# Node attention: remainders on GpSimd, fold and sines in a head's first step, one share product on ScalarE, masks on two groups of rows

## The reference, cut to what matters

```python
logits = (x @ wr).reshape(B, N, H, K_NODES).transpose(0, 2, 1, 3)
tk_vals, tk_idx = jax.lax.top_k(logits, TOP_K)
tk_w = jax.nn.softmax(tk_vals, axis=-1)
member = jax.nn.one_hot(tk_idx, K_NODES).sum(axis=-2) > 0
pos = jnp.cumsum(m_i, axis=2) - m_i                 # m_i: member as int
for n in range(K_NODES):
    c, s = cos_c[pos[..., n]], sin_c[pos[..., n]]
    qr = q * c + _rotate_half(q) * s
    kr = k * c + _rotate_half(k) * s
    scores = jnp.einsum('bhid,bhjd->bhij', qr, kr) * SCALE
    scores = jnp.where(causal & member[..., n][:, :, None, :], scores, NEG)
    outs.append(jnp.einsum('bhij,bhjd->bhid', jax.nn.softmax(scores, axis=-1), v))
gathered = jnp.take_along_axis(jnp.stack(outs, axis=3), tk_idx[..., None], axis=3)
y = (tk_w[..., None] * gathered).sum(axis=3)
```

## Time and profile before

| What | Before |
|---|---|
| median of 3 runs | 1853.75 us |
| runs | 1850.45 to 1855.61 us |
| the profiled execution's own time | 1856.05 us |
| its span | 1854.3 us |
| mean granted TensorE clock | 0.855 |
| busy: PE / DVE / ACT / POOL | 1372.8 / 1114.4 / 714.3 / 384.8 us |
| steps of the node attention | from 54 to 492 us |
| DVE busy from 102 to 158 us | 52.09 of 56 us |
| PE, ACT, POOL busy there | 48.56, 35.23, 34.30 us |

### The profile page before, as it was taken

One profiled execution on the slowest core, in us unless ns is written; L12 is line 12 of the kernel. 1 busy time (PEld: TensorE's weight loads), 2 busy tenths in 40 slices (PEclk: granted clock), 3 DMA queues, 4 the chain that ended last, 5 costly groups with the idle time before them and its releaser, 6 DMA issues. The chain is left out here.

```text
span 1854.3 us, 24940 instructions
## 1 busy us (share of the span) xinstructions
PE 1372.8 (74%) x8853; PEld 1037.9 (56%) x8853; DVE 1114.4 (60%) x2412; ACT 714.3 (39%) x1537; POOL 384.8 (21%) x400
## 2 busy tenths in 40 slices
PE   4898898888866897674674975758735977868785
PEld 3676666666745565561453964545623764744662
DVE  5899998999545576324556536443436648435634
ACT  4456666656313464232231221004102425645451
POOL 2565566665210100110101310000001000000000
PEclk8899899998878799796786986759967997989897
DMA  6011011010010100340002510000020002000100
GB/s 219 22 42 38 25 42 36 27 42 15 1 59 1 35 1 1 122 137 0 1 13 76 173 52 1 1 1 1 1 91 0 1 1 44 2 1 5 40 2 12
DMA packets 31611, 63.97 MB, mean 35 GB/s; under 512 B 6785, under 2 KB 18177, under 8 KB 30977
## 3 DMA queue, kind: packets, MB, share of 16 engines
q1 hardware_dynamic: 30464, 60.15, 10.5%
q0 software_dynamic: 1024, 2.23, 0.5%
HBM read 54.13 MB, written 4.18 MB: 31 GB/s over the span
## 5 line engine op out<-in xcount | busy, mean ns | idle before, releaser
L188 POOL TENSOR_TENSOR rstd<-spread,minus_half 128x4 f32<-128x4 f32 x36 | 36.8, 1023 | 1001.9 <-DVE spread L170 1001.9
L918 PE MATMUL l0h_scores<-l0h_k_rot,l0h_q_slots 128*128 128x128 f32 (+1 forms) x1024 | 206.6, 349 | 0.0
L918 PEld LDWEIGHTS l0h_scores<-l0h_k_rot,l0h_q_slots 128*128 128x128 f32 x1024 | 169.9, 208 | 13.1
L1135 POOL TENSOR_TENSOR l0h_k_part<-large_weights,l0h_sines 128x512 f32<-128x512 f32 x64 | 83.9, 1311 | 177.2 <-PE l0h_scores L918 129.1
L1009 ACT ACTIVATE l0h_scores<-l0h_scores,l0h_top 128x128 f32<-128x128 f32 (+1 forms) x256 | 100.4, 392 | 27.9 <-DVE l0h_top L1088 27.7
L1082 DVE TENSOR_TENSOR l0h_q_slots<-l0h_q_rot,l0h_chosen 128x1024 f32<-128x1024 f32 x64 | 78.4, 1225 | 6.7
L894 PE MATMUL l0h_projected<-XT,l0h_wq 128*128 128x256 f32 x256 | 70.2, 398 | 15.3 <-ACT large_weights L980 12.0
L908 PE MATMUL l0h_scores<-l0h_key_masks,l0h_query_picks 4*128 4x128 bf16 (+1 forms) x256 | 45.0, 257 | 49.2 <-DVE l0h_probs L1105 49.1
L1136 POOL TENSOR_TENSOR l0h_k_rot<-large_weights,l0h_cosines 128x512 f32<-128x512 f32 x64 | 80.9, 1264 | 0.0
L1088 DVE TENSOR_REDUCE l0h_top<-l0h_scores 128x2 f32<-128x256 f32 (+1 forms) x128 | 65.1, 548 | 6.4 <-PE l0h_scores L918 6.4
L1447 ACT ACTIVATE l0n_probs<-l0n_scores,l0n_top 128x256 f32<-128x256 f32 x128 | 53.8, 483 | 39.0 <-DVE l0n_top L1478 38.9
(11 more groups left out here) (762 smaller groups left out, 3585.8 us busy)
## 6 DMA issues: line engine op xcount, KB each, us to landing
l1e_experts<-in_l_experts SPq DMA_DIRECT2D x16, 768.0 KB, 4.3
l0e_experts<-in_l_experts SPq DMA_DIRECT2D x15, 578.0 KB, 4.0
l0h_chosen<-l0h_chosen_dram SPq DMA_DIRECT2D x64, 128.0 KB, 2.9
small_weights<-in_w_l_ffn SPq DMA_DIRECT2D x1, 4016.0 KB, 12.1
l0h_pos<-l0h_pos_dram SPq DMA_DIRECT2D x56, 64.0 KB, 2.0
large_weights<-in_w_l_xattn SPq DMA_DIRECT2D x1, 2632.0 KB, 9.0
l3f_late<-l3f_values SPq DMA_DIRECT2D x2, 1040.0 KB, 7.0
l0h_wq<-in_l_wq SPq DMA_DIRECT2D x16, 128.0 KB, 2.9
```

Source lines behind the costliest of these rows:

```text
L918: mm = nc.tensor.matmul(at[:, slot], q_slots[:, s % 2, slot, part, i * P:(i + 1) * P], k_rot[:, s % 2, part, 0:KEYS[i][1]], start=False, s ...
L1135: nc.gpsimd.tensor_tensor(k_part[:], source, at_batch(sines, s), ALU.mult)
```

## The change

Four edits, all in `l0_attn_heads`.

1. `reduce_turns` moves from VectorE to GpSimd for heads 2 to 15. Its place is behind `rotate_k(s)` in the first step of a head (b = 0), for head h+1; before, VectorE did it after step b = 3 for head h+2. Heads 0 and 1 stay on VectorE, ahead of the loop.
2. ScalarE does `fold(h+1)` right ahead of `sines_of(h+1)` at b = 0 and no longer at b = 3.
3. `combine` is split. `find_share(s)` (reciprocal and share) stands ahead of the slot product, which becomes `pick_slots(s+2)`. The first slot's product becomes two ScalarE copies with the share as scale, `scale_first(s)`, behind `exponents(s)` and ahead of `copy_out` and `copy_turned`. VectorE's second product waits for each of them. The two semaphores for this are ones that later attention stages use too, so their bases are raised.
4. `key_masks` and `query_picks` exist twice, at partitions 0 to 3 and 64 to 67, with a DMA each. The four mask products of a step are all issued ahead of the causal masks, with the two tiles, on different rows, taking turns.

```diff
-                    sp.dma_start(key_masks[:, h % 2], absent_dram[h * NODES:(h + 1) * NODES])\
...
+                    for i in range(TB):
+                        sp.dma_start(key_masks[rows_of_tile(i), h % 2], absent_dram[h * NODES:(h + 1) * NODES])\
+                            .then_inc(masks_loaded[h % 2], 16)
...
-                    pe.wait_ge(masks_loaded[h % 2], 32 * (h // 2 + 1))
+                    pe.wait_ge(masks_loaded[h % 2], 64 * (h // 2 + 1))
+                    for slot in range(CHOICES):
+                        for i in range(TB):
+                            query = slice((TB * b + i) * P, (TB * b + i + 1) * P)
+                            rows = rows_of_tile(i)
+                            nc.tensor.matmul(unit(scores, s, i)[:, slot], query_picks[rows, h % 2, slot, query],
+                                             key_masks[rows, h % 2, b * S:b * S + KEYS[i][1]], start=(slot == 0),
+                                             stop=False, skip_group_check=True)
...
+                def scale_first(s):
+                    act.wait_ge(shared, s + 1)
+                    if s >= 2:
+                        act.wait_ge(turned_ready, s - 1)
+                    for i in range(TB):
+                        nc.scalar.activation(prob(s, i), unit(scores, s, i)[:, 0], ACT.Copy,
+                                             scale=share[:, s % 2, i, 0:1]).then_inc(scaled, 1)
...
                     exponents(s)
+                    scale_first(s)
...
                     if b == 0 and 1 <= h < H0 - 1:
+                        fold(h + 1)
                         sines_of(h + 1)
                     if b == 2 and h + 2 < H0:
                         turns(h + 2)
-                    if b == 3 and h + 2 < H0:
-                        fold(h + 2)
...
+                def find_share(s):
                     h, b = step(s)
                     v.wait_ge(exp_ready, 2 * (s + 1))
                     link(v, nc.vector.reciprocal(inverse(s), total[:, s % 2]))
...
+                def combine(s):
                     for i in range(TB):
+                        v.wait_ge(scaled, 2 * s + i + 1)
+                        last = nc.vector.scalar_tensor_tensor(prob(s, i), unit(scores, s, i)[:, 1],
+                                                              share[:, s % 2, i, 1:2], prob(s, i), ALU.mult, ALU.add)
...
                     find_top(s)
                     if s + 2 < STEPS:
                         rotate_q(s + 2)
+                    find_share(s)
+                    if s + 2 < STEPS:
+                        pick_slots(s + 2)
                     combine(s)
-                    if b == 3 and h + 2 < H0:
-                        reduce_turns(h + 2)
...
+                def reduce_turns(h):
+                    g.wait_ge(turns_ready, h + 1)
+                    link(g, nc.gpsimd.tensor_scalar(sines[:, h % 2], cosines[:, h % 2], ROUND, ROUND, ALU.add, ALU.subtract))
+                    nc.gpsimd.tensor_tensor(sines[:, h % 2], sines[:, h % 2], cosines[:, h % 2], ALU.subtract)\
+                        .then_inc(turns_reduced, 1)
...
                 for s in range(STEPS):
+                    h, b = step(s)
                     rotate_k(s)
+                    if b == 0 and 1 <= h < H0 - 1:
+                        reduce_turns(h + 1)
```

More of the change, by code:

```diff
@@ L789, in l0_attn_heads @@
         chosen = sb("chosen", [P, 2, CHOICES, N], BF16)
-        key_masks = sb("key_masks", [NODES, 2, N], BF16)
-        query_picks = sb("query_picks", [NODES, 2, CHOICES, N], BF16)
+        key_masks = sb("key_masks", [P // 2 + NODES, 2, N], BF16)
+        query_picks = sb("query_picks", [P // 2 + NODES, 2, CHOICES, N], BF16)
+        rows_of_tile = lambda i: slice(i * P // 2, i * P // 2 + NODES)
         cosines, sines = sb("cosines", [P, 2, N]), sb("sines", [P, 2, N])
@@ L817, in l0_attn_heads @@
         inverse = lambda s: scores[:, s % 2, CHOICES * P:CHOICES * P + TB * CHOICES].rearrange("p (i o) -> p i o", i=TB)
+        share_ready, first_scaled = k.counted("attention", "shifted out_used")
+        shared, scaled = share_ready.sem, first_scaled.sem
+        prob = lambda s, i: probs[:, s % 2, i * P:i * P + KEYS[i][1]]
         with nc.Block() as block:
@@ L902, in score @@
                         pe.wait_ge(combined, s - 1)
-                    pe.wait_ge(masks_loaded[h % 2], 32 * (h // 2 + 1))
+                    pe.wait_ge(masks_loaded[h % 2], 64 * (h // 2 + 1))
[6 more added lines that the diff above has]
+                                             stop=False, skip_group_check=True)
                     for i in range(TB):
                         at = unit(scores, s, i)
-                        query = slice((TB * b + i) * P, (TB * b + i + 1) * P)
-                        for slot in range(CHOICES):
-                            nc.tensor.matmul(at[:, slot], query_picks[:, h % 2, slot, query],
-                                             key_masks[:, h % 2, b * S:b * S + KEYS[i][1]], start=(slot == 0), stop=False,
-                                             skip_group_check=True)
                         nc.tensor.matmul(at[:, :, i * P:(i + 1) * P], k.above[:], bc(k.masker[:].unsqueeze(1), [P, 2, P]),
@@ L1079, in rotate_q, with pick_slots @@
                     nc.vector.tensor_tensor(q_rot[:, 1], q_rot[:, 1], q_part[:, 0], ALU.add).then_inc(q_rotated, 1)
+                def pick_slots(s):
                     v.wait_ge(chosen_loaded[step(s)[0] % 2], 64 * (step(s)[0] // 2 + 1))
@@ L1089, in find_top @@
                             .then_inc(topped, 1)
-                def combine(s):
+                def find_share(s):
                     h, b = step(s)
@@ L1094, in combine @@
                     link(v, nc.vector.reciprocal(inverse(s), total[:, s % 2]))
-                    link(v, nc.vector.tensor_tensor(share[:, s % 2], inverse(s), mix[:, TB * b:TB * b + TB, h, :],
-                                                    ALU.mult))
-                    if s >= 2:
-                        v.wait_ge(turned_ready, s - 1)
-                    prob = lambda i: probs[:, s % 2, i * P:i * P + KEYS[i][1]]
-                    for i in range(TB):
-                        last = nc.vector.tensor_scalar(prob(i), unit(scores, s, i)[:, 0], share[:, s % 2, i, 0:1], None,
-                                                       ALU.mult)
-                    link(v, last)
-                    for i in range(TB):
-                        last = nc.vector.scalar_tensor_tensor(prob(i), unit(scores, s, i)[:, 1], share[:, s % 2, i, 1:2],
-                                                              prob(i), ALU.mult, ALU.add)
+                    nc.vector.tensor_tensor(share[:, s % 2], inverse(s), mix[:, TB * b:TB * b + TB, h, :], ALU.mult)\
+                        .then_inc(shared, 1)
+                def combine(s):
+                    for i in range(TB):
+                        v.wait_ge(scaled, 2 * s + i + 1)
+                        last = nc.vector.scalar_tensor_tensor(prob(s, i), unit(scores, s, i)[:, 1],
+                                                              share[:, s % 2, i, 1:2], prob(s, i), ALU.mult, ALU.add)
                     last.then_inc(combined, 1)
@@ L1110, in _ @@
                 reduce_turns(1)
-                rotate_q(0)
-                rotate_q(1)
+                for s in range(2):
+                    rotate_q(s)
+                    pick_slots(s)
                 for s in range(STEPS):
@@ L1145, in _ @@
                 for s in range(STEPS):
+                    h, b = step(s)
                     rotate_k(s)
+                    if b == 0 and 1 <= h < H0 - 1:
+                        reduce_turns(h + 1)
+        share_ready.base += STEPS
+        first_scaled.base += TB * STEPS
 HX, DX = 16, P // 16
```

7 lines of the change are left out of this document (3 added, 4 removed).

## The result

The changed kernel takes 1944.35 us (median of 6 runs, 1938.92 to 1947.96) against 1851.62 of six runs of the kernel before on the same chip: a ratio of 1.0485, 95% interval 1.0467 to 1.0503. It is slower, as forecast, but by 93 us and not by 31, and outside the range. Its profiled execution took 1945.9 us with a span of 1943.9, 89.6 more than before, at a mean granted clock of 0.828 against 0.855.

The account below looks back on a forecast made before the run. VectorE's 6.17 us step was taken to bound the kernel. After the change, 14 heads of 27.9 us through four queues plus 2.2 for the clock, 6.6 for heads 3, 7, 11, less 5.5 elsewhere: +30.7, about 1884 us, range 1846 to 1910.

Parts of the forecast that it names:

- VectorE's step: VectorE's own work per node attention step: from 6.17 us to 5.2, with ScalarE's two copies costed at nothing.
- The masks: TensorE's four mask products, on different rows by pairs, overlap partly: 0.15 us off an iteration.
- TensorE's turn: TensorE's score, weigh and turn at b = 2 end at T + 4.5 us; T is the end of combine(4h-3).
- The remainders: GpSimd's reduce_turns, held until turns is made: tensor_tensor 2.35 us plus tensor_scalar 1.0, together 3.4 us.
- Score, weigh, turn: TensorE's rest of score(4h+1), weigh and turn, after its stall for the rotated k: about 4.05 us with hand-over.
- The clock: Falls to 1.2 GHz behind TensorE's idle stretch cost 2.2 us a head; bounds 0, and 4 with a second fall.
- ScalarE's block: ScalarE's copy 0.5 us, fold 1.0, then first table load through sines to the reciprocal awaiting exponents, 6.45.
- TensorE's wait for combine: TensorE, done with its next iteration at T + 23.85 us, idles until T + 27.9: 4.0 us in every head.
- Outside the 14 heads: The six other full steps (0, 1, 58 to 61) gain 0.9 us each: -5.5 us.
- Rival 1: The turn through the queues holds but the clock's falls cost nothing: +0.2 us, 1854; chance 0.08.
- Rival 2: GpSimd's remainders don't hold up rotate_k: 25.45 us a head, 1850 us with the clock's 2.2, 1819 without; chance 0.16.
- Rival 3: Slower still: tensor_scalar at 2.35 us adds 19 us, a second clock fall up to 25: 1903 to 1928; chance 0.14.

Follow-up runs that it names:

- e12: The changed kernel with the split of combine undone, the first share product on VectorE again behind the slot product: 1947.86 us.
- e11: The changed kernel with only turns(h + 2) on ScalarE moved from b = 2 to b = 1: 1848.92 us.
- e2: The changed kernel with the remainders (reduce_turns) still on GpSimd but one step later, at b = 1 instead of b = 0: 1838.11 us.
- e7: The kernel before with only the doubled masks and their new order added: 1845.71 us against 1856.19.
- e4: The changed kernel with GpSimd's tensor_scalar cut from add and subtract to one multiplication, leaving out the rounding: 1939.88 us.
- e13: The changed kernel with unused TensorE products in both waits, 16 ahead of the masks of b = 1's score, 14 ahead of a head's first projection: 1908.15 us.
- e3: The changed kernel with unused TensorE products in both waits, 16 behind the masks of b = 1's score, 14 ahead of a head's first projection: 1900.38 us.
- e1: The changed kernel with the remainders (reduce_turns) back on VectorE behind step b = 3: 1868.5 us.
- e5: The changed kernel with only the 16 unused TensorE products ahead of the masks of b = 1's score, in the wait for k_rot: 1934.56 us.
- e6: The changed kernel with only the 14 unused TensorE products ahead of the projection of a head's first step: 1926.08 us.
- e8: The kernel before with the split of combine and the doubled masks, remainders and fold left at b = 3: 1842.35 us against 1856.19.

## Why the prediction was right in its sign and wrong in its size

The mechanism of the forecast holds: a loop through four queues, which VectorE enters only with the 2.2 us from reciprocal to combine's end (e12), which the changed kernel's timelines show link by link, and which e11 and e2 open by moving a single step. Point by point:

- **VectorE's step**: forecast 5.2 us, measured 5.07. ScalarE's two copies were costed at nothing: VectorE waited 0.9 us for them in all. Right.
- **The masks**: forecast 0.15 us off an iteration, measured 0.3 (e7).
- **TensorE's turn** at T + 4.5 was T + 6.7: 2.2 us, which is the clock's fall at half speed and belongs to its term.
- **The remainders**, forecast 3.4 us: 6.0. This is the first failed step, "It reads one input, not two, so I take 1.0". The tensor_tensor was right to 5 ns (2350 and 2345), the tensor_scalar 3.63. Not only the value chosen was off: the upper bound, a tensor_tensor at 2.35, was none. A two-input operation bounds a one-input one only if the inputs set the price. e4 shows that the operations do too, and that one operation alone is above the bound. 2.63 us x 14 = 37 us.
- **rotate_k** 4.0 us: 249.35 to 253.31. Right. The idle stretch of TensorE in front of it was 5.23 us in place of 2.65, and 2.65 + 2.63 = 5.28: by the dearer remainders. This is the path that the prediction had, with one link longer.
- **Score, weigh, turn** in 4.05: 5.7, the second fall.
- **The clock**, forecast +2.2 us a head with 4 kept as the bound "if the 2.65 us stall draws a second fall": the stall did, at 5.23 us. e13 against the change gives 4.0 us in each ordinary head. This is the second failed step: a term of 2.2 that should have been 4.0, 1.8 x 14 = 25 us. In heads 3, 7 and 11 no run measured it by itself, since there the added products cost time of their own. They take 35.6, 38.8 and 35.6 us; the forecast 27.9 + 2.2 + 2.2 = 32.3 and the 2.63 leave 0.6, 3.8 and 0.6, in the mean 1.7. In head 7 the clock is at 1.2 GHz for some 7 us behind each of its waits, in the other two for some 3.
- **ScalarE's block** from table load to reciprocal, 6.45 us: 260.63 to 267.08, 6.45. The copy and the fold before it, 1.5: 259.07 to 260.63. Reciprocal to T + one turn, 2.3: 2.2. Right.
- **TensorE's wait for combine**, 4.0 us: 4.26. Right.
- **Outside the 14 heads**: forecast -5.5, measured -8.0.

The two failed steps add up on the links. Forecast +30.7; the tensor_scalar adds 37 and the clock 25, outside gains 2.5 more, and 30.7 + 37 + 25 - 2.5 = 90, against 89.6 on the spans. As prices of their own they don't come apart: e4 took 0.86 us off the tensor_scalar and got 0.25 a head back in ordinary heads, since more of the clock's fall then lay on work. So the 37 us say where the time stands in the changed kernel, not what a cheaper tensor_scalar would give back.

The rivals. Rival 1, the falls cost nothing, is out by e3 and e13. Rival 2, GpSimd's remainders don't hold up rotate_k, is out by e2: 106 us go when they stand a step later. Its price was nearly right as a price of something else: it put 25.45 us on a head without that link and without the clock, and in e2 and e11 ordinary heads run at 25 to 28, with falls of the clock among them. Rival 3 had the mechanism, both of its parts came, and it still ended at 1928, because its first part was capped at the bound that failed. What I gave 0.14 should have had more: the two terms are linked, since dearer remainders lengthen the very stall that draws the second fall, and I had weighed them as if they were apart.

The Trainium skill (GPSIMD Engine Reference, 3.1) puts a one-input body at 1.03 cycles an element. By it the tensor_scalar would be an estimated 0.9 us; the rows give 3.63 with two operations and 2.77 with one, and the measurement decides. Its advice in the same section to keep elementwise work on VectorE agrees with the sign: 3.63 against 0.83 for the same instruction. But e2 beside e1 shows that breaking it can pay: with the same order on ScalarE the kernel with the remainders on GpSimd, behind rotate_k of b = 1, takes 30 us less than the one with them on VectorE.

## What to carry to other kernels

Where work moves to another engine's queue, follow one turn of the loop that the queues close, from the producer's place in its queue to the consumer's and back; free time on the receiving engine says nothing when the moved step stands there waiting with other work behind it. If such a step waits in every turn, move its producer earlier or itself later, by one step, before judging the change: that was worth 95 and 106 us here, more than any other single edit to the change. And bound the price of an instruction form that the trace doesn't have by more than the nearest form's, above all where a longer stall brings a second cost with it. Such costs don't add up like prices: after shortening one link, read the head again.

## What the runs showed of the hardware

- GpSimd's tensor_scalar with two operations, float32 in and out: 3.34 ns a column plus 0.21 us (3.63 us for 1024, 1.92 for 512); with one operation (multiply) 2.77 us for 1024. Its two-input tensor_tensor takes 2.35, so here fewer inputs isn't less time. All 14 took 3629 to 3651 ns, whatever VectorE did beside them.
- Each idle stretch of TensorE of 4.26 or 5.23 us in this loop drew a fall of the granted clock to 1.2 GHz, also when two stood in one head of 34 us. The fall outlasted the wait: in the changed kernel and in e4 the clock is 0.50 over the whole of 250.50 to 256.50, with the work back at 253.37 and at 252.19. With TensorE at work in both stretches the clock was 1.00 from 230 to 270 us (e3, e13), and 0.98 over 80 to 560 (e13) against 0.82. It took both (by the last reciprocal e5 and e6 gave 11 and 16 us, e13 40).
- VectorE and GpSimd lengthen each other where they overlap (e8, the rows above): VectorE's tensor_scalar took 1.62 us and its tensor_tensor 1.63, where the two that run alone at the start of the changed kernel take 0.69 and 1.22, and GpSimd's tensor_tensor 1.71 for 0.73. The Trainium skill (SBUF — State Buffer, Who interferes with whom) calls the port pair that the two share an exclusive lock, held for a whole instruction. These rows agree: if each of the three began only when the other engine's instruction had ended, they would show 1.76, 1.76 and 1.84 us, each 0.13 us above the measured one. Not every overlap does this: in the changed kernel VectorE's slot product at 250.25, which reads q_rot from PSUM, keeps its 1.22 us beside GpSimd's product at 250.57, which keeps its 1.26.
- In e3 the 16 products with their start flag stand behind the masks, in the same bank, and the scores come out without some of them; in e13 the same products stand ahead of the masks, and they don't. That it is the flag is argued from these two outputs; no trace shows it.
